# Attention phase of a conditioned sequence block: tokens turned by TensorE, a new order within a pair of batch rows, other DMA queues

## The reference

```python
xn = _layernorm(x, ln1_w, ln1_b)
xn = _modulate(xn, shift_a, scale_a)          # x * (1 + scale) + shift, one pair per sequence
q = (xn @ wq + bq).reshape(B, S, H, hd).transpose(0, 2, 1, 3)
k = (xn @ wk + bk).reshape(B, S, H, hd).transpose(0, 2, 1, 3)
v = (xn @ wv + bv).reshape(B, S, H, hd).transpose(0, 2, 1, 3)
scores = jnp.einsum('bhqd,bhkd->bhqk', q, k) / math.sqrt(hd)
attn = jax.nn.softmax(scores, axis=-1)
out = jnp.einsum('bhqk,bhkd->bhqd', attn, v)
x = residual + (out.transpose(0, 2, 1, 3).reshape(B, S, D) @ wo + bo)
```

## Time and profile before

| | |
|---|---|
| median of 3 runs | 2146.94 us (2146.7 to 2151.45) |
| profiled execution | 2152.45 us, span 2150.7 us |
| mean granted TensorE clock | 0.974 of 2.4 GHz |
| busy share of the span | TensorE 92%, weight loads 75%, VectorE 59%, ScalarE 35%, GpSimd 18% |
| attention phase, TensorE | first product at 776.2 us, first of the next phase at 1434.3 us |
| DMA | 293 MB, 136 GB/s over the span, about 207 GB/s in the attention |

### The profile page before, as it was taken

The page is one execution under the profiler, slowest core; times in us unless marked ns, Lnnn a source line. Parts: engine busy times, 40 slices in busy tenths (PEclk is TensorE's granted clock), DMA queues, the critical chain, the costliest instruction groups (busy, mean ns, idle before and its releaser), DMA issues. The chain is left out here.

```text
span 2150.7 us, 31443 instructions
## 1 busy us (share of the span) xinstructions
PE 1986.4 (92%) x10058; PEld 1615.2 (75%) x10058; DVE 1260.2 (59%) x2094; ACT 752.8 (35%) x2232; POOL 389.4 (18%) x491
## 2 busy tenths in 40 slices
PE   6899999999999988888888888859999999999999
PEld 4678888887888866767767767647888888888887
DVE  6567767767677756667666676645525345253422
ACT  3223332233222336566466565633212122121211
POOL 4223332322222211111111111101101011010200
PEclk8999999999999999999999999979999999999999
DMA  8444444544445436666667666652202102021000
GB/s 304 141 164 156 149 137 161 172 150 152 135 155 174 142 104 207 198 198 217 211 196 224 200 209 215 191 196 84 74 5 79 49 30 78 0 78 54 24 20 20
DMA packets 262154, 293.08 MB, mean 136 GB/s; under 512 B 17261, under 2 KB 179657, under 8 KB 262089
## 3 DMA queue, kind: packets, MB, share of 16 engines
q1 hardware_dynamic: 250568, 258.12, 37.1%
q0 software_dynamic: 9360, 29.96, 4.7%
q10 hardware_dynamic: 2160, 4.20, 0.6%
HBM read 175.29 MB, written 100.14 MB: 128 GB/s over the span
## 5 line engine op out<-in xcount | busy, mean ns | idle before, releaser
L617 PE MATMUL mlp_y<-weights,mlp_h 128*128 128x512 f32 x1536 | 382.9, 400 | 15.1 <-DVE mlp_h L854 14.2
L617 PE MATMUL ffn_y<-weights,ffn_h 128*128 128x512 f32 x1536 | 377.5, 395 | 3.0 <-DVE ffn_h L854 3.0
L594 PE MATMUL mlp_m<-xn,weights 128*128 128x512 f32 x1536 | 370.0, 392 | 5.6 <-DVE xn L842 5.6
L594 PE MATMUL ffn_m<-xn,weights 128*128 128x512 f32 x1536 | 370.8, 391 | 2.4 <-PEq L145 2.4
L617 PEld LDWEIGHTS mlp_y<-weights,mlp_h 128*128 128x128 f32 x1536 | 291.1, 190 | 88.4 <-issue 9.8
L617 PEld LDWEIGHTS ffn_y<-weights,ffn_h 128*128 128x128 f32 x1536 | 288.1, 188 | 72.7 <-DVE ffn_h L854 4.3
L594 PEld LDWEIGHTS mlp_m<-xn,weights 128*128 128x128 f32 x1536 | 289.4, 189 | 69.3 <-DVE xn L842 6.0
L594 PEld LDWEIGHTS ffn_m<-xn,weights 128*128 128x128 f32 x1536 | 289.4, 188 | 65.3 <-issue 2.9
L730 ACT ACTIVATE ffn_g<-ffn_m,vecs 128x512 f32<-128x512 f32 x128 | 88.1, 688 | 553.6 <-PE ffn_m L594 549.4
L852 DVE CAST ffn_h<-ffn_g 128x512 fp32r<-128x512 f32 x128 | 57.6, 450 | 378.2 <-ACT ffn_g L730 377.5
L1300 PE MATMUL att_banks<-xn,weights 128*128 128x256 f32 x1536 | 211.5, 299 | 35.4 <-DVE xn L1558 28.7
(11 more groups left out here) (128 smaller groups left out, 2081.2 us busy)
## 6 DMA issues: line engine op xcount, KB each, us to landing
x_tiles<-x SPq DMA_DIRECT2D x132, 256.0 KB, 3.5
turned_probs<-att_probs SPq DMA_DIRECT2D x64, 512.0 KB, 3.3
x<-x_tiles SPq DMA_DIRECT2D x96, 256.0 KB, 3.4
mlp_bias<-gate_bias_rows POOLq DMA_DIRECT2D x64, 256.0 KB, 3.9
att_kdiag<-xn SPq DMA_DIRECT2D x128, 128.0 KB, 3.0
probsT_room<-turned_probs SPq DMA_DIRECT2D x64, 256.0 KB, 3.1
x_tiles<-turned_probs SPq DMA_DIRECT2D x64, 256.0 KB, 3.2
turned_squares<-mlp_xhat SPq DMA_DIRECT2D x62, 256.0 KB, 3.3
```

What stands on the lines that cost most here:

```text
L594: last = nc.tensor.matmul(m1_ps[:, c % 2, :], st.tiles[0](a, k, c), xn[:, parity, b, k, :], start=s == 0, stop=s == len(steps) - 1)
L617: last = nc.tensor.matmul(y_ps[:, tile, :], h[:, c % 2, a, tile * P:(tile + 1) * P], st.tiles[1](b, c), start=c == 0 and s == 0, stop=c == ...
```

## The change

Four things change in `attention_phase`, and with the second all the others move.

1. **Turning.** `normalise` writes the tile back in place with no transpose behind it, and `turn` on TensorE turns it in four 128x128 transposes against the identity, into bank 1 or 2 of the score banks (`turn_bank`). `modulate` reads that bank. `store_squares` and `load_squares` are gone. Since the banks are those of the scores, `turn(n + 1, tile)` waits for exponentials of the pair before, and `scores(n, 0, e)` wait for `modulate(n + 1, e)`.
2. **Order of a pair.** Each `pair_step` is written anew.
3. **Probabilities.** On SP the two stores of a tile's halves no longer alternate each with its own load and with other waits; the loads of both halves follow the second store. The first store of a pair stands at the end of its step, the second at the start of the next.
4. **Token loads.** `load_x` is issued by GpSimd, between the four `negative_max`; the wait of `load_piece` is now for the piece before it.

`schedule` now unrolls two steps ahead of the first pair, pairs 0 and 1, pairs 14 and 15, and two steps behind the last. In the diff below, cut to its core, the four new `pair_step` are shown with their added lines alone; those removed stand above, in the kernel before.

```diff
+        score_bank = lambda m: s_ps[:, m * HPC:(m + 1) * HPC, :].rearrange("p h k -> p (h k)")
+        project_bank = lambda tile: (score_bank(0), bank_ps[:, 1, :])[tile]
+        turn_bank = lambda tile: score_bank(tile + 1)
...
+        def schedule(eng, first, pair_step):
             first()
+            for n in range(-2, 2):
+                pair_step(n)
+            with eng.Fori(0, NPAIR - 4) as i:
+                pair_step(i + 2)
+            for n in range(NPAIR - 2, NPAIR + 2):
+                pair_step(n)
...
+            def pair_step(n):
+                if is_pair(n - 1):
+                    store_probs(n - 1, 0, 1)
+                    load_probs(n - 1, 0, 0)
+                    load_probs(n - 1, 0, 1)
+                if is_pair(n - 2):
+                    store(n - 2, 1)
+                if is_pair(n - 1):
+                    store_probs(n - 1, 1, 0)
+                if is_pair(n):
+                    diag(n, 0)
+                if is_pair(n - 1):
+                    store_probs(n - 1, 1, 1)
+                    load_probs(n - 1, 1, 0)
+                    load_probs(n - 1, 1, 1)
+                if is_pair(n):
+                    diag(n, 1)
+                if is_pair(n - 1):
                     load_residual(n - 1, 1)
                     store(n - 1, 0)
+                if is_pair(n):
+                    store_probs(n, 0, 0)
+                    load_residual(n, 0)
...
+            def load_x(n, tile):
+                if is_next(n):
+                    rows = following.source[TPP * (n - NPAIR) + tile]
+                else:
+                    rows = source_t[TPP * n + tile]
+                if n == 1:
+                    pool.wait_ge(loads_open, 1)
+                else:
+                    pool.wait_ge(xn_ready, tiles_before(n - 1, tile) + 1)
+                if is_next(n):
+                    pool.wait_ge(stored[tile], 16 * (n - NPAIR + 1))
+                pool.dma_start(x[:, tile, :], rows).then_inc(x_loaded[tile], 16)
...
+            for n in range(-2, NPAIR + 2):
+                if is_pair(n):
+                    negative_max(n, 0, 0)
+                    negative_max(n, 0, 1)
+                if is_pair(n - 1):
+                    add_bias(n - 1, 1)
+                if is_pair(n):
+                    negative_max(n, 1, 0)
+                if is_pair(n + 1):
                     load_piece(n + 1)
+                if is_turned(n + 2):
+                    load_x(n + 2, 0)
+                if is_pair(n):
+                    negative_max(n, 1, 1)
+                if is_turned(n + 2):
+                    load_x(n + 2, 1)
+                    rstd_of(n + 2, 0)
+                if is_pair(n):
+                    add_bias(n, 0)
+                if is_turned(n + 2):
+                    rstd_of(n + 2, 1)
...
+                if u == 0 and not is_first(n):
+                    pe.wait_ge(xn_ready, TPP * n)
+                    pe.wait_ge(v_ready, TPP * n)
+                if u == 1 and is_pair(n - 2):
+                    pe.wait_ge(x_final, TPP * (n - 1))
+                if u >= 3:
+                    pe.wait_ge(kq_ready, 2 * KC * n + u - 2)
...
+                    pe.wait_ge(modulated, tiles_before(n + 1, e) + 1)
+                if tile == 0 and e == 0 and is_pair(n - 1):
+                    pe.wait_ge(x_final, TPP * (n - 1) + 1)
...
+            def turn(n, tile):
+                pe.wait_ge(xhat_ready, tiles_before(n, tile) + 1)
+                if is_pair(n - 2):
+                    pe.wait_ge(exp_done, 4 * (n - 1) - 1 + tile)
+                for k in range(KC):
+                    last = nc.tensor.transpose(turn_bank(tile)[:, k * P:(k + 1) * P], x[:, tile, k * P:(k + 1) * P], sh.ident[:, :])
+                last.then_inc(turned, 1)
...
+            def pair_step(n):
+                if is_pair(n):
+                    for u in (1, 2, 3, 4):
+                        keys_queries(n, u)
+                if is_pair(n - 1):
+                    weigh(n - 1, 0)
+                if is_pair(n):
+                    keys_queries(n, 5)
+                    keys_queries(n, 6)
+                if is_turned(n + 1):
+                    turn(n + 1, 0)
+                if is_pair(n - 1):
+                    project(n - 1, 0)
+                if is_first(n):
+                    value_bias_product()
+                if is_pair(n):
+                    keys_queries(n, 7)
+                if is_turned(n + 1):
+                    turn(n + 1, 1)
+                if is_pair(n):
+                    scores(n, 0, 0)
+                    scores(n, 0, 1)
+                    values(n, 0)
+                    values(n, 1)
+                if is_pair(n - 1):
+                    weigh(n - 1, 1)
+                if is_pair(n):
+                    scores(n, 1, 0)
+                    scores(n, 1, 1)
+                if is_pair(n - 1):
+                    project(n - 1, 1)
+                if is_pair(n + 1):
+                    keys_queries(n + 1, 0)
...
                 row = TPP * n + tile
-                act.wait_ge(squares_loaded, 16 * (swaps(n, tile) + 1))
...
-                    last = nc.scalar.activation(part, part, ACT.Identity,
+                    last = nc.scalar.activation(xmod[:, tile, k, :], turn_bank(tile)[:, k * P:(k + 1) * P], ACT.Identity,
                                                 bias=sh.tables[:, place, 1, k, bass.ds(row, 1)], scale=sh.tables[:, place, 0, k, bass.ds(row, 1)])
                 last.then_inc(modulated, 1)
...
+            def pair_step(n):
+                if is_pair(n):
+                    kq_high(n, 0)
+                if is_pair(n - 1):
+                    exponentials(n - 1, 1, 1, FIRST_HEADS)
+                if is_pair(n):
+                    kq_high(n, 1)
+                    kq_high(n, 2)
+                    kq_high(n, 3)
+                if is_pair(n - 1):
+                    exponentials(n - 1, 1, 1, LAST_HEADS)
+                if is_pair(n):
+                    kq_high(n, 4)
+                if is_pair(n - 1):
+                    out_high(n - 1, 0)
+                    divide(n - 1, FIRST_HEADS)
+                if is_pair(n):
+                    kq_high(n, 5)
+                if is_pair(n - 1):
+                    divide(n - 1, LAST_HEADS)
+                if is_pair(n):
+                    piece_high(n)
+                    kq_high(n, 6)
+                if is_turned(n + 1):
+                    modulate(n + 1, 0)
+                if is_pair(n):
+                    kq_high(n, 7)
+                if is_turned(n + 1):
+                    modulate(n + 1, 1)
+                if is_pair(n):
+                    exponentials(n, 0, 0, ALL_HEADS)
+                    exponentials(n, 0, 1, ALL_HEADS)
+                    copy_values(n, 0)
+                if is_pair(n - 1):
+                    out_high(n - 1, 1)
+                if is_turned(n + 1):
+                    x_high(n + 1, 0)
+                    x_high(n + 1, 1)
+                if is_pair(n):
+                    copy_values(n, 1)
+                    exponentials(n, 1, 0, ALL_HEADS)
...
-                dve.wait_ge(rstd_done, swaps(n, tile) + 1)
-                if not (isinstance(n, int) and n == 1 and tile == 0):
-                    dve.wait_ge(squares_stored, 16 * swaps(n, tile))
-                if tile == 0 and not (is_next(n) and n > NPAIR):
-                    dve.wait_ge(piece_done, n)
-                nc.vector.tensor_scalar(stage[:, :].rearrange("p (q k i) -> p q k i", q=NSQ, k=KC),
-                                        x[:, tile, :].rearrange("p (k i q) -> p q k i", k=KC, q=NSQ),
-                                        mv[:, tile, 0:1], rstd[:, tile:tile + 1], ALU.subtract, ALU.mult).then_inc(xhat_ready, 1)
-                dve.wait_ge(xhat_ready, swaps(n, tile) + 1)
-                nc.vector.transpose(stage[:, :], stage[:, :]).then_inc(squares_turned, 1)
+                dve.wait_ge(rstd_done, tiles_before(n, tile) + 1)
+                nc.vector.tensor_scalar(x[:, tile, :], x[:, tile, :], mv[:, tile, 0:1], rstd[:, tile:tile + 1],
+                                        ALU.subtract, ALU.mult).then_inc(xhat_ready, 1)
...
+            def pair_step(n):
+                if is_pair(n):
+                    kq_low(n, 0)
+                if is_pair(n - 1):
+                    divide(n - 1, 1, 0)
+                if is_pair(n):
+                    kq_low(n, 1)
+                if is_pair(n - 1):
                     turn_probs(n - 1, 1, 0)
+                if is_pair(n):
+                    kq_low(n, 2)
+                    kq_low(n, 3)
+                if is_turned(n + 1):
+                    stats(n + 1, 0)
+                if is_pair(n - 1):
+                    invert(n - 1, 1, 1)
+                    out_low(n - 1, 0)
+                if is_turned(n + 1):
+                    normalise(n + 1, 0)
+                if is_pair(n):
+                    kq_low(n, 4)
+                if is_turned(n + 1):
+                    stats(n + 1, 1)
```

(55 more changed lines are left out.)

352 lines of the change are left out of this document (71 added, 281 removed).

## The result

The changed kernel takes 2041.93 us (median of 4 runs, 2038.54 to 2044.03) against 2146.82 us for the kernel before. The ratio is 0.9508, with a 95% interval from 0.9487 to 0.9528: 105 us faster, where 75 were forecast.

What follows compares the result with a forecast made beforehand. A pair was bound by the loop through ScalarE and DMA, not TensorE. 32.24 work, 1.2 turns, 0.3 at (a) and 0.9 hand-offs gave 34.6 us a pair; 75 us less in all, median 2072, range 2051 to 2104.

Steps and rivals of the forecast that it cites:

- 32.24 us of TensorE's work: Attention loop: TensorE's work in a pair whose clock never fell, taken as the base of the new pair.
- Turns, 1.2 us a pair: TensorE's added transposes, eight a pair: 0.6 us a turn, 1.2 us a pair, bounds 0.8 and 2.0.
- (a): Second score half waits for modulate(n + 1, 1), so TensorE waits some 0.3 us a pair.
- Hand-offs that the walk can't see, 0.9 us: Per pair, unseen hand-offs between engines: 0.9 us, chosen as about a third of today's shortest waits together.
- (b): Exponentials of tile 0 start at about 3.7 us; tile 1's score half needing them stands at 10.3, 4 us to spare.
- (c): VectorE's chain from out_low to x_low: xn ready at 15.6 us, key product wants it at 16.2; tightest place, 0.6 us.
- (d): project of tile 0 has 3.6 us of work before it against out_high and out_low's 1.3; the 0.74 us wait goes.
- Probabilities, 3 us hidden: Tile 0's last probability load lands at 21 us, its weigh stands at about 24; three microseconds hide it.
- Token loads, hidden: GpSimd's own DMA lands after 3.9 us, statistics are taken some 9 us after issue of the later tile; hidden.
- the clock did not fall: Rival: TensorE's clock falls in the attention pairs, 37.8 us each, 2117 us, or 2094 at half; chance 0.18.
- VectorE's bound at (c): Rival: VectorE's chain before the key product is 1.5 us longer than counted; pair 36 us, total 2092; chance 0.15.
- Probabilities too late in every pair: Rival: SP's order makes weigh wait in every pair, slower than before; 2170 us at 9 us lateness; chance 0.02.

Runs made afterwards that it cites:

- the early turn: Changed kernel with the second token tile's turn ahead of the pair's last key and query product, its modulate ahead of that product's kq_high: 2041.06 us, ratio 0.9515.

## Why the prediction was wrong in size, step by step

The direction was right, and so was the mechanism: the squares' way through DRAM and what stood behind it set the pair, and without it and in the new order TensorE sets it at full clock. The forecast of 2072 was 30 us too high, and 2041.93 lies below the range's lower end, 2051. The steps:

- **"32.24 us of TensorE's work" is the step that failed.** It was taken from a stretch with five idle pieces (of 0.65 to 1.94 us in TensorE's timeline) and the end of a sixth, and used as a floor (33.1 with the least that a turn could cost). Without any idle piece, the pair's work with its turns is 31.43 us, so 30.7 without them (31.43 less 2 x 0.36). The runs show the reason: the same work reads 31.43 us busy with no idle piece, 31.61 with one and 31.87 with two, so each adds 0.18 to 0.26 us to what is shown as busy. Five of them make an estimated 0.9 to 1.3 of the 1.5 us; what the rest is, no run shows. In the kernel before, 39.0 us held 8.3 us of standing still, not 6.8. I added durations where I should have subtracted starts. The Trainium skill (Perfetto Trace Analysis, Tensor Engine Instruction) says that a matmul's reported end is computed from its size and a delay and not observed. The 2.92 us of a group whose successor starts after 2.76 agrees.
- **Turns, 1.2 us a pair:** 0.72 measured. The opening's 0.66 held the same excess, at a clock of 0.91. The 0.42 of weight loads, named as the least that a turn can cost, was nearer but no floor: a turn took 0.36.
- **(a), 0.3 us:** 0.54, the period of 31.97 less 31.43. Right in kind, though too small.
- **Hand-offs that the walk can't see, 0.9 us:** none. A third of today's shortest waits was a guess, with no row of this order behind it.
- **(b), 4 us to spare:** right. The eighth exponential of tile 0 ends near 954.3, its score half starts at 958.22. **(c), 0.6 us:** 0.75, `x_low` done at 963.14 before the key product at 963.89. That it is as tight as that is shown by the early turn, which lost there what it had won at (a). **(d)**: no wait.
- **Probabilities, 3 us hidden:** right in eleven of twelve pairs, but tighter than 3 us. In the pair shown the last load of tile 0 is issued at 964.6 and lands after 6.1 us (I had some 4), at 970.7, and `weigh` reads it at 971.63: 0.9 us hide it. The decision of SP's order was worth 8 us elsewhere, and had been given nothing.
- **Token loads, hidden:** right. GpSimd's issues took 0.54 to 0.59 us each, and the run that gives them back to SP is level. They land after 5.3 us (median) where I had 3.9, within the slack. The starving of a DMA from GpSimd that the Trainium skill (SBUF — State Buffer) describes was not seen to cost anything; whether it is in the 5.3 us no run shows.

For a pair the four terms give 34.6 - 1.5 - 0.5 + 0.2 - 0.9 = 31.9 us. Over thirteen pairs that is 34 us of the attention's 42 that I missed. The rest: pair 1 took 33.4 us where I had 37, pair 15 31.8 and not 34.6, the first pair 30.65 and not 32.8, the tail 27.87 and not 29; the one late `weigh` gave 1.8 back. Of that, 9.0 us were lost again in the last phase: 6.9 us of stalls and 3.7 of slower work behind them, less 1.6 of other waits. In the two profiled executions the untouched first phase gave 6.3 us, and they stand 5.5 above and 3.4 below their medians, which brings the 42 to the 30 of the medians. "Nothing is left to win" there was right, but nothing was allowed for what the phase could lose by standing elsewhere in memory.

The rivals: the clock did not fall, not with the turns doubled and not with an idle piece added. The Trainium skill's rule that transposes do not count as work (TensorE: Matmul & The Clock Gate, Part 4) is neither shown nor refuted, since 0.72 us and even 1.6 us of them a pair left the clock at 1.00. VectorE's bound at (c) did not bind, by 0.75 us. Probabilities too late in every pair did not occur.

## What to carry to other kernels

Price a tightly packed stretch by the distance between starts in a stretch that already has no waits; the busy time of a stretch with idle pieces is too high, here by some 0.2 us for each. When a wait on the critical engine is taken away and nothing is gained, look at which of two instructions on VectorE and GpSimd now begins first. And before a gain or loss of some 8 us is put down to an edit, look at the untouched phases behind it: compare their waits and the packets of the instruction queue, shift the code and measure again.

## What the hardware showed that I had not expected

Two stalls of about 3.5 us each in an untouched phase came and went with the number of TensorE instructions ahead of it: 6.3 to 6.9 us in four kernels, at most 1.6 in the others, and some 3.7 us more of busy time behind them, where the clock read 0.50. The same loop had its code brought again in each round in some programs (17 blocks over two rounds) and not in others (at most one). VectorE's multiply and GpSimd's addition excluded each other for the whole of an instruction, so that a shift of 0.5 us in their order took 0.8 us from one engine and gave 0.9 to the other. And a busy time grew by 0.26 us when TensorE merely waited once more.
